# A decoder block on one core: the state-space scan laid out as units of 32 channels x 4 states

## The reference

```python
# 1: state-space layer, 256 channels, 16 states, per sequence b and token l
xs, res = split(x @ W_in)                    # 256 + 256
u = silu(conv4(xs) + conv_b)                 # causal, per channel
x_dbl = u @ W_x                              # 64 (low rank of delta) + 16 (B) + 16 (C)
delta = softplus(x_dbl[..., :64] @ W_dt + b_dt)
h[l, c, n] = exp(delta[l, c] * A[c, n]) * h[l-1, c, n] + delta[l, c] * u[l, c] * B[l, n]
y = sum_n h[l, c, n] * C[l, n] + u * D
x = layernorm(x + (y * silu(res)) @ W_out)
# 2: causal attention, 16 heads of 8, rotary q and k, keys and values from the context
x = layernorm(x + attention(x, ctx, mask) @ Wo.T + bo)
# 3: 8 experts of 512, two chosen for each token
x = layernorm(x + experts(x))
```

## Time and profile before

| | |
|---|---|
| median of 3 runs | 1165.22 us (1157.1 to 1165.36) |
| the profiled execution, its own time | 1163.2 us |
| its span, first to last instruction | 1161.4 us |
| busy PE, DVE, ACT, POOL | 1022.0, 804.3, 759.5, 600.3 us |
| mean granted TensorE clock | 0.962 |

### The profile page before, as it was taken

The page is one execution under the profiler, slowest core; times in us unless marked ns, Lnnn a source line. Parts: engine busy times, 40 slices in busy tenths (PEclk is TensorE's granted clock), DMA queues, the critical chain, the costliest instruction groups (busy, mean ns, idle before and its releaser), DMA issues.

```text
span 1161.4 us, 19208 instructions
## 1 busy us (share of the span) xinstructions
PE 1022.0 (88%) x5287; PEld 562.4 (48%) x5288; DVE 804.3 (69%) x1625; ACT 759.5 (65%) x2101; POOL 600.3 (52%) x388
## 2 busy tenths in 40 slices
PE   6799889989988988988899887977945999999987
PEld 2344544544454454445445534532533666666662
DVE  1597798788679868867986796798653544444437
ACT  2778877967786777679676775964742444444446
POOL 2595277278627936872794487379132333322210
PEclk9899999999899999999998999998987999999999
DMA  4000000000100000010000000000422111111134
GB/s 113 6 5 24 6 1 10 19 1 1 39 9 1 18 29 2 0 37 11 1 16 22 1 1 29 1 1 9 154 101 56 42 41 41 41 43 44 41 100 145
DMA packets 39402, 36.56 MB, mean 31 GB/s; under 512 B 6561, under 2 KB 35361, under 8 KB 38945
## 3 DMA queue, kind: packets, MB, share of 16 engines
q1 hardware_dynamic: 33792, 25.99, 7.7%
q0 software_dynamic: 4352, 8.99, 2.2%
q10 hardware_dynamic: 1184, 0.70, 0.3%
HBM read 23.99 MB, written 11.67 MB: 31 GB/s over the span
## 4 chain that ended last, share of the span: by engine, by line
PE 62%; ACT 14%; DVE 10%; issue 7%; POOL 4%; DMA 2%; SPq 1%; another core or an unknown queue 0%; DVEq 0%; POOLq 0%; ACTq 0%
PE y_ps L1339 13%; ACT prob L623 8%; PE bank L1616 6%; PE bank L1630 6%; PE bank L1617 6%; PE bank L1261 5%; DVE scan L861 4%; PE bank L1424 3%; PE y_ps L1622 3%; POOL hc_pool L427 2%; PE bank L1433 2%; PE bank L1457 2%; PE bank L1315 2%; PE bank L1326 1%; PE bank L1360 1%
## 5 line engine op out<-in xcount | busy, mean ns | idle before, releaser
L420 POOL TENSOR_TENSOR scan<-du,w 128x1024 f32<-128x1024 f32 x128 | 298.8, 2358 | 153.0 <-PE y_ps L1424 88.1
L861 DVE TENSOR_TENSOR_SCAN scan<-bank,scan 128x512 f32<-128x512 f32 x240 | 282.1, 1209 | 22.1 <-ACT bank L588 20.6
L588 ACT ACTIVATE bank<-delta,a_neg 128x512 f32<-128x512 f32 x240 | 163.5, 691 | 54.0 <-DVE scan L861 52.6
L1339 PE MATMUL y_ps<-w,ident 128*128 128x512 f32 x352 | 166.9, 596 | 0.0
L498 POOL DMA_INDIRECT y<-aoT,dest x72 | 69.2, 962 | 172.9 <-DVE aoT L1193 166.2
L868 DVE TENSOR_TENSOR w<-scan,bank 128x1024 f32<-128x1024 f32 x88 | 106.1, 1206 | 16.4 <-DVE scan L861 6.8
L571 ACT ACTIVATE w<-bank 128x512 f32<-128x512 f32 x121 | 71.3, 589 | 69.1 <-PE bank L1315 67.1
L1152 DVE TENSOR_TENSOR zpos<-zabs,bank 128x512 f32<-128x512 f32 x74 | 50.8, 687 | 78.8 <-PE bank L1617 77.7
L1339 PEld LDWEIGHTS y_ps<-w,ident 128*128 128x128 f32 x352 | 68.0, 193 | 62.0 <-issue 57.3
L623 ACT ACTIVATE prob<-y_ps,nmax 128x128 f32<-128x128 f32 x256 | 91.2, 430 | 0.4 <-DVE nmax L930 0.4
L623 ACT ACTIVATE prob<-bank,nmax 128x128 f32<-128x128 f32 x256 | 89.8, 387 | 2.2 <-DVE nmax L930 2.2
(11 more groups left out here) (257 smaller groups left out, 2057.4 us busy)
## 6 DMA issues: line engine op xcount, KB each, us to landing
qk<-xg SPq DMA_DIRECT2D x79, 65.0 KB, 1.9
cn<-in_ctx SPq DMA_DIRECT2D x8, 256.0 KB, 2.9
mask_b<-in_mask SPq DMA_DIRECT2D x8, 256.0 KB
w<-in_w1T SPq DMA_DIRECT2D x1, 2048.0 KB, 8.8
w<-in_w3T SPq DMA_DIRECT2D x1, 2048.0 KB, 7.7
prob<-in_w2T SPq DMA_DIRECT2D x1, 2048.0 KB
u<-y SPq DMA_DIRECT2D x4, 512.0 KB, 5.9
w<-in_x SPq DMA_DIRECT2D x6, 256.0 KB, 3.0
```

Source lines behind the costliest of these rows:

```text
L420: g_.tensor_tensor(bu[:, n % 3], du[:, :, :], b_row[:, n % 3, :].unsqueeze(1).broadcast_to((P, 2, T)), ALU.mult).then_inc(s["bu_sb"], 1)
L588: A(bank[(6 if n else 4) + h], delta[:, h, :], ACT.Exp, scale=a_neg[:, h, n:n + 1]).then_inc(s["a_ps"], 1)
L861: v_.tensor_tensor_scan(hst[:, n % 3, h, :], bank[(6 if n else 4) + h], bu[:, n % 3, h, :], 0.0, ALU.mult, ALU.add).then_inc(s["h_sb"], 1)
L1339: last = MM(y_ps[:, h], ident[:, :], hc_pool[:, h, :] if n in POOLED else hc[:, ON_DVE.index(n) % 3, h, :], start=False, stop=False, skip_ ...
```

## The change

The scan is now a loop over NU = 16 units `k`. A unit is 32 channels x 4 states on the partitions (partition 32j + c holds channel c, state j of a quarter `q`), and its 1024 columns are 2 sequences x 4 quarters of the states x 128 tokens. Units 0 to 7 are the 8 blocks of 32 channels for sequences 0 and 1, units 8 to 15 the same for 2 and 3.

- B: `b_columns` gives B with tokens on partitions, and POOL makes a diagonal matrix of it for each state, in blocks of 64 tokens (`diagonals`). `du_t` transposes delta * u. PE multiplies the two (`entries`): two parts of eight fp32 matmuls, 64 rows x 32 columns, 256 wide, each on its own tile of the array; the result is in the scan's layout in PSUM. The rows of B, the selector matmuls and the three bf16 parts are gone.
- Delta and C: `delta` and the rows of C are stored to DRAM and loaded back, repeated over partitions, as `delta_rep` (four times) and `c_rep` (32 times), by DMAs on SP's queue.
- ACT: four exponentials of 256 columns per unit, to SBUF (`decay`).
- DVE: one scan of 1024 columns per unit, in a ring of eight places; the last unit's product with C too.
- POOL: products with C in place for 15 units (`times_c`), the sums of `add_q`, and in the middle of the scan the next group's delta and du.
- PE: sums over states in four batches (`y_add`): 16 fp32 matmuls with a 128x32 matrix of ones, 256 wide, four tiles of 32 columns.
- Order: since sequences 0 and 1 are done after unit 7, their gate, W_out, norm, transposes, queries and rope stand between the units 9 to 14. The silus of group `c` stand after the key copies and before the first exponentials. Six warming matmuls in each group are gone (`keep_warm(6)`), banks are shared out anew, and more buffers have a place of their own.

```diff
+            def delta_out(m):
+                at(sp, "delta_set", m + 1)
+                sp.dma_start(d_dram[m].rearrange("(h p) t -> p h t", h=2), delta[:, :, :]).then_inc(s["delta_store"], 16)
...
+            def delta_in(m, r):
+                at(sp, "delta_store", 16 * m + 16)
+                at(sp, "decay_sb", NU * (m - 1) + NB * (r + 1))
+                for j in range(4):
+                    sp.dma_start(delta_rep[32 * j:32 * j + 32, :, toks[r]],
+                                 d_dram[m].rearrange("(b c) t -> c b t", b=NB)[:, :, toks[r]]).then_inc(s[f"delta_load{r}"], 16)
...
-            def times_b(m, n):
...
+            def diagonals(m, r):
+
+                at(pool, "btok_sb", m + 1)
+                at(pool, "bu_ps", NU * (m - 1) + NB * (r + 1))
+                for t in (2 * r, 2 * r + 1):
+                    last = g_.tensor_tensor(b_diag[:, t], diag64[:, :].unsqueeze(1).broadcast_to((P, NST, HK)),
+                                            b_tok[:, t, :].unsqueeze(2).broadcast_to((P, NST, HK)), ALU.mult)
+                last.then_inc(s["bdiag_sb"], 1)
+
+            def times_c(m, k):
+                r = k // NB
+                at(pool, "h_sb", NU * m + k + 1)
+                at(pool, f"c_load{r}", 64 * m + 64)
+                g_.tensor_tensor(by_state(ring(k)), by_state(ring(k)),
+                                 c_rep[:, :, toks[r]].rearrange("p q (i t) -> p i q t", i=2), ALU.mult).then_inc(s["hc_sb"], 1)
...
+            def decay(m, k, qs):
+                r, b = divmod(k, NB)
+                at(act, f"delta_load{r}", 64 * m + 64)
+                at(act, "h_sb", NU * m + k - 1)
+                for q in qs:
+                    last = A(by_state(decays[:, k % 2, :])[:, :, q, :], delta_rep[:, b, toks[r]].rearrange("p (i t) -> p i t", i=2), ACT.Exp,
+                             scale=a_neg[:, q, b:b + 1])
...
+                own_k(g, 2)
+                own_k(g, 3)
+                if e is not None:
+                    duT_out(e, 1, 6)
                 if c is not None:
                     silus(c)
...
+                exps(g, 0, 0)
...
+            def states(m, k):
+                at(dve, "decay_sb", NU * m + k + 1)
+                at(dve, "bu_ps", NU * m + k + 1)
+                at(dve, "y_sum", 4 * m + k // 4 - 1)
...
+                v_.tensor_tensor_scan(ring(k), decays[:, k % 2, :], pair(k)[:, :, :].rearrange("p i c -> p (i c)"), 0.0, ALU.mult, ALU.add).then_inc(s["h_sb"], 1)
...
+            def entries(m, k, part):
+
+
+                r, b = divmod(k, NB)
+                if part:
+                    at(pe, "bu_half", NU * m + k + 1)
+                elif k > 2:
+                    at(pe, "h_sb", NU * m + k - 1)
...
+                at(pe, "bdiag_sb", 2 * m + r + 1)
+                at(pe, "duT_sb", 2 * m + r + 1)
+                for i in range(2):
+                    z = i ^ part
+                    half = slice(HK * z, HK * z + HK)
+                    for j in range(4):
+                        last = MM(pair(k)[32 * j:32 * j + 32, i, :].rearrange("p (q z t) -> p q z t", q=NQ, z=2)[:, :, z, :],
+                                  du_tok[half, r, i, 32 * b:32 * b + 32], b_diag[half, 2 * r + i, j::4, :], start=True, stop=True)
+                last.then_inc(s["bu_ps" if part else "bu_half"], 1)
...
+            def y_add(m, x):
...
+                for q in range(NQ):
+                    for i in range(4):
+                        last = MM(y_ps[32 * i:32 * i + 32, r, h * HT:(h + 1) * HT].rearrange("p (i t) -> p i t", i=2), sum32[:, :],
+                                  by_state(ring(4 * x + i))[:, :, q, :], start=False, stop=(q == NQ - 1), skip_group_check=True)
+                last.then_inc(s["y_sum"], 1)
```

PE's list for a group, without the lines that only go:

```diff
+                for k in range(1, NU):
+                    ahead = k + 1 < NU
+                    if ahead:
+                        entries(m, k + 1, 0)
+                    if k == 1:
                         y_begin(m)
...
+                        if k == 4:
+                            x2_t(w)
+                        if k == 5:
                             logits(w)
...
+                        if k == 5:
+                            b_columns(e)
+                        if k == 6:
+                            step(e, 1, 7)
...
+                        if k in (7, 8):
+                            conv(c, 0, (2 * k - 14,), 6)
+                        if k in (11, 12):
+                            conv(c, 1, (2 * k - 21,), 6)
+                    if k == 9:
+                        values(g)
+                    if k == 10:
+                        residual(g, 0)
+                    if k == 13:
+                        x1_t(g, 0)
+                    if k == 14:
+                        queries(g, 0)
+                    if ahead:
+                        entries(m, k + 1, 1)
+                    if k in (5, 9, 13):
+                        y_add(m, k // 4 - 1)
+                    if e is not None:
+                        if k == 4:
+                            low_steps(e, 6)
+                        if k == 5:
+                            step(e, 0, 6)
+                        if k == 7:
+                            c_rows(e, 7)
+                        if k == 14:
+                            du_t(e, 0, 6)
+                    if c is not None:
+                        if k == 6:
+                            x_t(c, 6)
+                        if k in (7, 8):
+                            conv(c, 0, (2 * k - 13,), 6)
+                        if k == 10:
+                            conv(c, 1, (0,), 6)
+                        if k == 11:
+                            conv(c, 1, (2,), 6)
+                        if k in (12, 13):
+                            res(c, k - 12, 6)
+                    if k == 11:
+                        first_out(g, 0)
+                if e is not None:
+                    du_t(e, 1, 6)
+                scores(g, 0, 0)
+                y_add(g, 3)
                 residual(g, 1)
+                scores(g, 0, 1)
                 first_out(g, 1)
```

857 lines of the change are left out of this document (401 added, 456 removed).

## The result

The changed kernel is slower: 1229.4 us median of 4 runs (1223.1 to 1234.3) against 1161.5 us for the kernel before (a fourth run beside the three above), a ratio of 1.058 [1.051, 1.066]. The forecast was 1104. On two other occasions the ratio was 1.064 [1.060, 1.069] and 1.053 [1.048, 1.058], and on one 1.033 [1.030, 1.037]; that one differs for a reason that the experiments bring out.

What follows compares the result with a forecast made beforehand. TensorE was taken to stay the scan stretch's bound. First group's last scan at 105 us, seven periods of 94 (658) less 3 give 760, plus 344 after the last scan: 1104 us; range 1045 to 1185.

Steps and rivals of the forecast that it cites:

- The open price, the entries: TensorE's B products in the scan: each part 0.43 us plus 0.27 for switches, 1.4 us per unit of two parts.
- A sum batch: TensorE's sums over states: 16 fp32 matmuls per batch in 1.9 us, 7.5 us per group instead of 27.5.
- GpSimd's strided products: GpSimd's products with operands read in short runs: 2.36 us each, at worst 1.4 times that.
- the exponentials start: Attention stretch: ScalarE's exponentials start 5.9 us after the last scan ends, instead of 16.
- the first scan: Kernel's start: first scan at 51 us instead of 40.33, as delta and C go through DRAM and back.
- The two rivals on row tiles: Entries: row halves don't overlap, a part 0.85 us, 1187 us, chance 0.12; partial overlap, 0.64, 1150 us, chance 0.12.
- the one on GpSimd: Scan stretch: GpSimd's strided products cost 1.4 times, 57 us per stretch, about 1150 us in all; chance 0.08.
- the 0.64: Entries part by the skill's 10.6 of 16 packing: 0.64 us, a period 6 us longer, 1150 us in all.
- the attention stretch's last steps: End of the attention stretch: decays, widening, scans, copy, norm and statistics, within 41.5 us from last scan to scan 2.
- the clock rival: Many small tiles might leave TensorE at 1.2 GHz in scans: +40 us per group, over 1300 us; chance 0.06.
- the periods: One group of four sequences: 52 us of scans plus 41.5 us of attention, 94 us against 102.
- The slots: Scan stretch, slots 1 to 14: the larger of TensorE and VectorE in each, summing to 52.6 us, taken as 52.

Runs made afterwards that it cites:

- experiment (28 + 12): Changed kernel with unit 1's entries ahead of the last heads, 1192.1 us (28); also with y's start and statistics moved out of slot 1, 1177.5 us (12).
- 6th session: Later measuring occasion without late results: kernel before 1135.2 us, changed kernel again 1175.5 us, ratio 1.033.
- the two repairs: Changed kernel with the attention's end reordered and y's start halved into TensorE's pauses, scatter burst left in the attention: 1181.1 us (5th session), 1124.8 us (6th).
- that best kernel: Changed kernel with attention's end reordered and y's start halved into the pauses, burst left in the attention: 1124.8 us, 0.992 of the kernel before.
- its repairs: Changed kernel with new order and filled pauses, burst left: 0.992 (6th session); with scatters also spread behind products of units 6 to 13: 0.994 (5th).
- spread kernels: Changed kernel with new order, y's start halves in the pauses and single scatters behind products of units 6 to 13: 1150.9 us, 0.992 (3rd session).
- two units earlier: Kernel with new order, filled pauses and spread scatters, those scatters moved behind the products of units 4 to 11: 1154.4 us, 1.016 (4th session).
- the second burst: Kernel with new order, filled pauses and spread scatters, plus all eight scatters reissued in one attention burst: 1152.9 us, 1.014 (4th session); 1154.6 us, 1.017 (6th).

## Why the prediction was wrong

**Right, by its own steps.** The open price, the entries, came out on the good side. TensorE's timeline, with other work between the parts:

```profile
191.05 0.66 PE L1371 MATMUL pair_b<-w,du_tok 64*32 64x256 f32 x16
191.64 1.13 PE L1286 MATMUL bank<-xT,w_conv 128*128 128x512 f32 x2
...
196.02 0.66 PE L1371 MATMUL pair_a<-w,du_tok 64*32 64x256 f32 x16
196.62 0.41 PE L1392 MATMUL y_ps<-hst,sum 128*32 128x256 f32 x2
...
198.48 0.66 PE L1371 MATMUL pair_b<-w,du_tok 64*32 64x256 f32 x16
```

A part with its switches takes 0.59 us (191.64 - 191.05) where 0.43 + 0.27 was allowed, one of two in a row 0.46 (from 157.41 to 157.87): row and column tiles multiply. A sum batch takes 1.86 us (from 196.62 to the next entries at 198.48; forecast 1.9), GpSimd's strided products 2.37 as forecast, DVE's scan 2.29, the exponentials start 5.4 us after the last scan ends (forecast 5.9), the first scan is at 49.7 (forecast 51). The two rivals on row tiles and the one on GpSimd fall. The Trainium skill (TensorE: Matmul & The Clock Gate, Part 3) gives 10.6 times instead of 16 for its finest packing; for these 2 x 4 tiles the trace shows 8 matmuls of 0.43 in 0.46, nearly all of the eightfold, so the 0.64 that I had estimated from it doesn't hold here.

**Wrong, first: the attention stretch's last steps.** The sum for it ends "then a unit's four decays 1.6 and a widening 0.2, scan 2.3, a copy 0.7, scan 2.3, norm and statistics 1.0". That is a chain of ACT's and DVE's durations; TensorE's list was never laid beside it. It holds half of unit 1's entries behind heads that wait for that very copy, and the start of y between the halves of unit 2's. 6.3 us became 11.6. The order costs 40 us by experiment (28 + 12), 44 by the two traces.

**Wrong, second: a moved step without a price.** The eight scatters went from the layer norm into the heads. The prediction has no term for them and no rival. The row was there to be found: matmul results up to 3.8 us late during the burst of the kernel before. In sessions with late results this is 8 us in each of five groups (47.7 against 39.6) and again 10 after the last scan (355.3 us from its end there, 345.5 in the same kernel in the 6th session), 51 us. As medians, the changed kernel is 45 to 60 us slower in such sessions than in the 6th, and the kernel before about 24. The hole is shown; what makes the results late is not. Without it the changed kernel is still slower than the kernel before: 1175.5 us in the 6th session, a ratio of 1.033.

**Wrong, third: the clock rival was right in kind.** I had put it on the tiles; it is the pauses of 1.3 us that the change leaves in slots 2 and 3. Filling them, at the price of 15 us of added work, gives back 11 us, not hundreds.

**Of the 125 us between forecast and measurement** the kernels themselves give this account: 54 us between the first and the 6th session (1229.4 and 1175.5, the same kernel), 51 us by the two repairs, order and pauses (1175.5 and 1124.8, both in the 6th session), and 21 us that are left there (1124.8 over 1104). The last 21 are the periods, 96.0 us on the mean where 93.6 was summed up (17 us in seven), and 4 us behind the last scan (347.6 where 344 was forecast). In a period, third to last scan takes 52.3 us or more instead of 49.7, and last to next first 38.7 to 40.4 instead of 37.6.

**The slots came out in their sum only.** The sum is 5% low, but single slots are off by up to 3.0 us. In that best kernel scans 6 and 7 lie 5.8 us apart where I had 2.8, scans 14 and 15 lie 5.2 apart where I had 3.1, and on the other side there are 2.4 in slot 4 for 3.6 and 2.8 in slot 13 for 4.6. The sums and most steps stand behind the second part of the entries in TensorE's list, so that what they cost falls in good part on the slot after. TensorE is busy for 48.0 of the 52.3 us, where the terms of the same slots add up to 45, although each unit's entries cost 0.2 us less than their term: the rest of its list was priced some 6 us too low.

**The size of the gain.** Taken with its repairs the change is worth 1%, not 5 (0.992 [0.988, 0.996] and 0.994 [0.991, 0.996]). TensorE does 54.6 us of work in the scan stretch, against 55.4 before: what the sums over states save (27.5 down to 7.5 us), the 32 parts of the entries and the rest spend again. DVE is relieved of 12 us (54.6 to 42.8), which doesn't shorten a stretch that TensorE fills.

## What to carry to other kernels

Where a change moves work across a boundary between stages, write down the list of every engine there in order, not one chain of durations: a step queued behind a wait on TensorE cost 5 us a group at nothing but a wrong place. A step that is only moved has a new neighbour: look in the old trace at what the others do while it runs, and compare modelled ends of matmuls with the moments their semaphores were raised. And run a kernel on more than one occasion before a few per cent of it are believed.

## What the runs showed of the hardware

- Bursts of indirect DMAs from GpSimd (1.26 us apart) go with results of TensorE that come up to 8 us late in the attention, in all four sessions with late results that ran one there (first, 2nd, 5th, 7th); plain DMAs from the same queue and rows (3rd session) don't. In 2 sessions of 7 nothing of the kind is in any of 5 traces, and the kernel before is 2% faster. What differs between sessions isn't known; the traces with late results also lack 13 to 72% of the scatters' landing records, the others at most one in 1024, and no run without recording is there to compare.
- Spreading the scatters one by one leaves 0.3 to 1.0 us of lateness each where results are late, and costs GpSimd's own time: where nothing is late, spread kernels have ratios of 1.016 (two units earlier) and 1.017 (with the second burst), and the one with the burst in the attention 0.992.
- From the second of two pauses of 1.3 us on the granted clock stood at its lower level, 1.2 GHz (0.50 from 163 to 169.5 us), and again from 173 to 180 us, with TensorE busy for all of those 7 us and of the 3.5 before; 15 us of needless matmuls in the pauses saved 11 us.
- Eight fp32 matmuls of 64 rows x 32 columns, 256 wide, on eight tiles of the array take 0.46 us in a row of such groups and 0.59 us between full-array matmuls.
